# The second norm's shift and scale, moved from the token rows to the transposed rows

## The reference

```python
mod = (silu(c) @ wmod).reshape(4, 6, 1, -1)          # one row of 128 per chunk, six kinds
sa, ca, ga, sb, cb, gb = mod[:, 0], ..., mod[:, 5]
h = layernorm(x) * (1 + ca) + sa
x = x + ga * attention_like(h)      # rmsnorm, gate and value, two depthwise convolutions, fuse, out
h = layernorm(x) * (1 + cb) + sb    # the second norm, with its modulation
x = x + gb * moe(h)                 # 160 experts, the 8 largest weighted, and a shared one
```

## Time and profile before

| | |
|---|---|
| median of 3 runs | 573.82 us (571.63 to 575.61) |
| the profiled execution, its own time | 573.52 us |
| its span, first to last instruction | 571.7 us |
| mean granted TensorE clock | 0.987 of full |
| PE busy | 544.1 us (95% of the span) |
| DVE busy | 474.0 us (83%) |
| ACT busy | 414.4 us (72%) |
| POOL busy | 29.6 us (5%) |

### The profile page before, as it was taken

The page is one execution under the profiler, slowest core; times in us unless marked ns, Lnnn a source line. Parts: engine busy times, 40 slices in busy tenths (PEclk is TensorE's granted clock), DMA queues, the critical chain, the costliest instruction groups (busy, mean ns, idle before and its releaser), DMA issues.

```text
span 571.7 us, 7315 instructions
## 1 busy us (share of the span) xinstructions
PE 544.1 (95%) x2528; PEld 251.4 (44%) x2528; DVE 474.0 (83%) x600; ACT 414.4 (72%) x668; POOL 29.6 (5%) x52
## 2 busy tenths in 40 slices
PE   5697889999999999999999999999989999999996
PEld 3334424543444444454444444454434444444442
DVE  5676479999959988799859688789959988999995
ACT  5446488789777776779666686568876877777773
POOL 5011000050000000011000000002000000000000
PEclk9797999999999999999999999999999999999999
DMA  7976075445534655455544455455635666566650
GB/s 265 346 258 263 10 248 180 150 150 179 185 110 148 204 187 176 146 169 199 158 138 148 170 185 174 148 181 188 213 119 180 231 201 203 198 207 205 200 186 18
DMA packets 33244, 103.26 MB, mean 181 GB/s; under 512 B 3700, under 2 KB 9013, under 8 KB 32952
## 3 DMA queue, kind: packets, MB, share of 16 engines
q1 hardware_dynamic: 33208, 102.81, 53.3%
HBM read 99.90 MB, written 2.37 MB: 179 GB/s over the span
## 4 chain that ended last, share of the span: by engine, by line
PE 78%; DVE 9%; ACT 5%; issue 4%; DMA 2%; POOL 1%; SPq 0%; ACTq 0%; DVEq 0%
PE bank L954 24%; PE bank L955 24%; PE bank L956 24%; DVE g_all L927 2%; DVE s_all L931 2%; PE bank L1075 2%; ACT g_all L667 1%; DMA c_all<-combine 1%; PE bank L1085 1%; DMA g_all<-wmod_dram 1%; ACT s_all L648 1%; DVE w L791 1%; PE bank L1150 1%; ACT hnT L594 1%; PE bank L1109 0%
## 5 line engine op out<-in xcount | busy, mean ns | idle before, releaser
L648 ACT ACTIVATE s_all<-bank 128x512 f32<-128x512 f32 x320 | 189.4, 593 | 109.6 <-PE bank L956 105.9
L927 DVE TENSOR_TENSOR g_all<-s_all,g_all 128x1024 f16<-128x1024 f32 x160 | 195.3, 1221 | 55.6 <-ACT g_all L667 55.1
L931 DVE TENSOR_TENSOR s_all<-s_all,c_all 128x1024 f32<-128x1024 f32 x160 | 194.8, 1218 | 3.9 <-DMA c_all<-combine 3.4
L667 ACT ACTIVATE g_all<-s_all 128x1024 f16<-128x1024 f32 x160 | 168.0, 1050 | 3.4 <-DVE s_all L931 3.3
L954 PE MATMUL bank<-x_h,w 128*128 128x512 f16 x320 | 121.4, 380 | 4.1 <-ACT s_all L648 4.0
L954 PE MATMUL bank<-g_all,w 128*128 128x512 f16 x320 | 121.4, 379 | 2.7 <-DVE g_all L927 2.7
L955 PE MATMUL bank<-g_all,w 128*128 128x512 f16 x320 | 121.3, 379 | 0.0
L956 PE MATMUL bank<-g_all,w 128*128 128x512 f16 x320 | 121.3, 379 | 0.0
L956 PE MATMUL bank<-x_l,w 128*128 128x512 f16 x320 | 121.3, 379 | 0.0
L955 PE MATMUL bank<-x_h,w 128*128 128x512 f16 x320 | 121.3, 379 | 0.0
L954 PEld LDWEIGHTS bank<-x_h,w 128*128 128x128 f16 x320 | 31.3, 98 | 46.9 <-ACT s_all L648 10.0
(11 more groups left out here) (212 smaller groups left out, 367.6 us busy)
## 6 DMA issues: line engine op xcount, KB each, us to landing
c_all<-combine SPq DMA_DIRECT2D x160, 512.0 KB, 3.9
w<-w_dram SPq DMA_DIRECT2D x20, 512.0 KB, 8.9
s_all<-mats_dram SPq DMA_DIRECT2D x1, 1152.0 KB, 7.6
attw<-symT_dram SPq DMA_DIRECT2D x1, 1152.0 KB, 10.3
res<-x_dram SPq DMA_DIRECT2D x4, 256.0 KB, 9.0
combine<-cT SPq DMA_DIRECT2D x4, 256.0 KB, 3.1
out_dram<-res SPq DMA_DIRECT2D x4, 256.0 KB, 2.4
mod<-rows_mod SPq DMA_DIRECT2D x1, 960.0 KB, 6.5
```

The costliest lines, as they stand in the source:

```text
L648: a(sr[J % SRING][:, q * L:(q + 1) * L], U[q][:], ACT.Silu, scale=1.0 / ES).then_inc(s["s_done"], 1)
L667: a(gh[n % GRING], sr[n % SRING], ACT.Copy).then_inc(s["hi_set"], 1)
L927: e.tensor_tensor(gl[n % GRING], sr[n % SRING], gh[n % GRING], ALU.subtract).then_inc(s["lo_set"], 1)
L931: e.tensor_tensor(sr[J % SRING], sr[J % SRING], cr[J % CRING], ALU.mult).then_inc(s["gm"], 1)
```

## The change

Rows 3 and 4 of mod (sb and cb) are no longer formed as rows: `MODC` falls from 5 x 128 to 3 x 128 columns, so the setup's wide matmuls and ACT copies are narrower and fewer, and the DMA through HBM carries 576 KB. sb and cb become columns, beside gb, by two more small matmuls; two small DVE instructions put them in SBUF (`sbc`, `cbc`, 1 added to cb). The steps `h2m` and `h2a` are gone. `xh` now has two ACTIVATEs that read TB with a scale and a bias per partition: one writes a float32 copy `x32`, the other `x_h`; `xl` subtracts in SBUF. In the tables `turn2` goes from 22 to 20, `xh` from 23 to 22, and the first convolution tap from 20 to 19.

```diff
-MODC = 5 * D
+MODC = 3 * D
 REST = {
...
-    17: ("t2a",), 18: ("t2b",), 19: ("h2m",), 20: ("h2a",), 22: ("turn2",), 23: ("xh",), 24: ("xl",), 26: ("logit", "shup"),
+    17: ("t2a",), 18: ("t2b",), 20: ("turn2",), 22: ("xh",), 24: ("xl",), 26: ("logit", "shup"),
...
-TAPS = {20: 1, 21: 1, 22: 1, 23: 1, 24: 1, 25: 1, 27: 2, 28: 2, 29: 1, 30: 1, 31: 1, 32: 1, 33: 1, 34: 1, 35: 1, 36: 1}
+TAPS = {19: 1, 21: 1, 22: 1, 23: 1, 24: 1, 25: 1, 27: 2, 28: 2, 29: 1, 30: 1, 31: 1, 32: 1, 33: 1, 34: 1, 35: 1, 36: 1}
...
     att(0, "t2b")
-    att(0, "h2m")
-    att(0, "h2a")
...
             def rows_of(b):
                 act.wait_ge(s["mod_ps"], 1)
-                a(mod[:, b, 0:512], U0[:], ACT.Copy).then_inc(s["mod_half"], 1)
-                act.wait_ge(s["mod_ps"], 2)
-                a(mod[:, b, 512:MODC], U1[:, 0:MODC - 512], ACT.Copy).then_inc(s["mod_half"], 1)
+                a(mod[:, b, :], U0[:, 0:MODC], ACT.Copy).then_inc(s["mod_half"], 1)
...
-                    a(x_h[b][:], TB[:], ACT.Copy).then_inc(s["xh_set"], 1)
+                    if c == 0:
+                        act.wait_ge(s["cb_set"], 2)
+                    else:
+                        act.wait_ge(s["xl_set"], c)
+                    a(x32[:], TB[:], ACT.Identity, bias=sbc[:, c:c + 1], scale=cbc[:, c:c + 1]).then_inc(s["x32_set"], 1)
+                    a(x_h[b][:], TB[:], ACT.Identity, bias=sbc[:, c:c + 1], scale=cbc[:, c:c + 1]).then_inc(s["xh_set"], 1)
...
-                dve.wait_ge(s["gb_ps"], 1)
+                dve.wait_ge(s["cols_ps"], 1)
+                e.tensor_copy(sbc[:], TB[:, B:2 * B]).then_inc(s["cb_set"], 1)
+                e.tensor_scalar(cbc[:], TB[:, 2 * B:3 * B], 1.0, None, ALU.add).then_inc(s["cb_set"], 1)
...
-                elif n == "h2m":
-                    for i in range(2):
-                        w = slice(2 * i, 2 * i + 2)
-                        dve.wait_ge(s["t2_set"], c * NT + 2 * i + 2)
-                        e.tensor_tensor(h0[:, w], h0[:, w], modr(c, 4, 2), ALU.mult).then_inc(s["hm_set"], 1)
-                elif n == "h2a":
-                    for i in range(2):
-                        w = slice(2 * i, 2 * i + 2)
-                        dve.wait_ge(s["hm_set"], 2 * c + i + 1)
-                        e.tensor_tensor(h0[:, w], h0[:, w], modr(c, 3, 2), ALU.add).then_inc(s["h2_set"], 1)
                 elif n == "xl":
                     b = c % 2
+                    dve.wait_ge(s["x32_set"], c + 1)
                     dve.wait_ge(s["xh_set"], c + 1)
...
-                    e.tensor_tensor(x_l[b][:], TB[:], x_h[b][:], ALU.subtract).then_inc(s["xl_set"], 1)
+                    e.tensor_tensor(x_l[b][:], x32[:], x_h[b][:], ALU.subtract).then_inc(s["xl_set"], 1)
...
-                mm(U0[:], scb[:, b, :], wmod[:, 0:512]).then_inc(s["mod_ps"], 1)
-                mm(U1[:, 0:MODC - 512], scb[:, b, :], wmod[:, 512:MODC]).then_inc(s["mod_ps"], 1)
+                mm(U0[:, 0:MODC], scb[:, b, :], wmod[:, 0:MODC]).then_inc(s["mod_ps"], 1)
...
-                    mm(TB[:, 0:B], wmod[:, MODC:], scb[:, :, 0]).then_inc(s["gb_ps"], 1)
-                    mm(A1[0:B, :], scb[:, :, 0], wmod[:, 0:512])
-                    mm(A2[0:B, 0:MODC - 512], scb[:, :, 0], wmod[:, 512:MODC]).then_inc(s["row_ps"], 1)
+                    mm(A1[0:B, 0:MODC], scb[:, :, 0], wmod[:, 0:MODC]).then_inc(s["row_ps"], 1)
+                    for i, j in enumerate((5, 3, 4)):
+                        last = mm(TB[:, i * B:(i + 1) * B], wmod[:, j * D:(j + 1) * D], scb[:, :, 0])
+                    last.then_inc(s["cols_ps"], 1)
...
-                            pe.wait_ge(s["h2_set"], 2 * c + t // 2 + 1)
+                            pe.wait_ge(s["t2_set"], c * NT + t + 2)
```

More of the change, by code:

```diff
@@ L253, in build @@
         gmag, gsgn = sb("gmag", [P, D]), sb("gsgn", [P, D])
-        gbc, gbm, gbs = (sb(n, [P, B]) for n in ("gbc", "gbm", "gbs"))
+        gbc, gbm, gbs, sbc, cbc = (sb(n, [P, B]) for n in ("gbc", "gbm", "gbs", "sbc", "cbc"))
         res = sb("res", [P, B * NT, D])
@@ L266, in build @@
         x_l = [sb(f"x_l{i}", [P, L], F16) for i in range(2)]
+        x32 = sb("x32", [P, L])
         ss32 = sb("ss32", [INTER, L])
@@ L315, in build @@
             "x_in0 x_in1 x_in2 x_in3 pool_zero pads zs_zero zs_one eps_set one_set scb_set mod_ps mod_half mod_set row_ps row_half row_set "
-            "gb_ps gb_set ak_set bm_set fold1 fold1_sb cols_set fold2 zb_set wz_hi wz_lo fold3 waf_hi waf_lo "
+            "cols_ps cb_set gb_set ak_set bm_set fold1 fold1_sb cols_set fold2 zb_set wz_hi wz_lo fold3 waf_hi waf_lo "
             "wb_ps wb_set sc_ps sc_hi sc_lo nws_set winf_set win_hi win_lo sym_set wc_hi wc_lo rr_set rsg_hi rsg_lo sdw_set table_set "
@@ L319, in build @@
             "conv_ps s_set gate_ps gate_set y_ps gy_set wo_set gob_set u_set gx_set base_set o_ps x2_set stats2 aggr2 ve2_set rstd2_set nb2_set "
-            "t2_set hm_set h2_set h2T_ps xh_set xl_set lg_ps pr_set sh_ps ss_set "
+            "t2_set h2T_ps xh_set x32_set xl_set lg_ps pr_set sh_ps ss_set "
             "mx_set rp_set cw_set sm_set sme_set rs_set cn_set cT_ps cT_set c_out "
@@ L389, in setup @@
                 if n == 20:
-                    sp.wait_ge(s["row_set"], 6)
+                    sp.wait_ge(s["row_set"], 5)
                     sp.dma_start(rowd.rearrange("o (b j) -> (o b) j", b=B - 1), row4[1:B]).then_inc(s["row_out"], 16)
@@ L523, in setup @@
                     act.wait_ge(s["row_ps"], 1)
-                    a(row4[:, 0:512], A1[0:B], ACT.Copy)
-                    a(row4[:, 512:MODC], A2[0:B, 0:MODC - 512], ACT.Copy).then_inc(s["row_half"], 1)
+                    a(row4[:], A1[0:B, 0:MODC], ACT.Copy).then_inc(s["row_half"], 1)
                 elif n == 4:
@@ L690, in gains @@
                 e.tensor_scalar(rw[:, 1, :], rw[:, 1, :], 1.0, None, ALU.add).then_inc(done, 1)
-                e.tensor_scalar(rw[:, 4, :], rw[:, 4, :], 1.0, None, ALU.add).then_inc(done, 1)
                 e.tensor_scalar(sgn, rw[:, 2, :], 0.0, 2.0, ALU.is_ge, ALU.mult).then_inc(done, 1)
-                dve.wait_ge(done, 3)
+                dve.wait_ge(done, 2)
                 e.scalar_tensor_tensor(out=mag, in0=sgn, scalar=-1.0, in1=rw[:, 2, :], op0=ALU.add, op1=ALU.mult)\
                     .then_inc(done, 1)
+                dve.wait_ge(done, 3)
+                e.tensor_scalar(mag, mag, 0.25, None, ALU.max).then_inc(done, 1)
                 dve.wait_ge(done, 4)
-                e.tensor_scalar(mag, mag, 0.25, None, ALU.max).then_inc(done, 1)
-                dve.wait_ge(done, 5)
                 e.scalar_tensor_tensor(out=rw[:, 2, :], in0=sgn, scalar=-1.0, in1=mag, op0=ALU.add, op1=ALU.mult)\
@@ L717, in setup @@
                     dve.wait_ge(s["ld_vec"], 16)
-                    dve.wait_ge(s["mod_half"], 2)
+                    dve.wait_ge(s["mod_half"], 1)
                     gains(mod[:, 0].rearrange("p (j d) -> p j d", d=D), gmag[:], gsgn[:], s["mod_set"])
@@ L772, in mod_ready @@
                 else:
-                    dve.wait_ge(s["mod_set"], 6)
+                    dve.wait_ge(s["mod_set"], 5)
             def gates():
-                dve.wait_ge(s["gb_ps"], 1)
+                dve.wait_ge(s["cols_ps"], 1)
+                e.tensor_copy(sbc[:], TB[:, B:2 * B]).then_inc(s["cb_set"], 1)
+                e.tensor_scalar(cbc[:], TB[:, 2 * B:3 * B], 1.0, None, ALU.add).then_inc(s["cb_set"], 1)
                 e.tensor_scalar(gbs[:], TB[:, 0:B], 0.0, 2.0, ALU.is_ge, ALU.mult).then_inc(s["gb_set"], 1)
@@ L1131, in duo @@
                 if J == 0:
-                    pe.wait_ge(s["mod_half"], 2)
+                    pe.wait_ge(s["mod_half"], 1)
                 if J < ALL and J % DUOS == 0:
```

## The result

| | before | after |
|---|---|---|
| median of 20 runs each | 572.83 us (571.31 to 575.61) | 576.35 us (573.77 to 579.66) |
| the profiled execution, its own time | 573.52 us | 578.59 us |
| its span | 571.7 us | 576.8 us |
| mean granted clock | 0.987 | 0.985 |

The account below looks back on a forecast made before the run. PE's order of work was taken to bound the loop, one chain through all engines the prologue. Setup -0.1, prologue xh +0.4, tap +1.85 and +1.4 gave +3.5 us on 573.5, so 577.0 us, range 573.2 to 581.5.

Parts of the forecast that it names:

- The bound: In the loop PE's order of work sets the time; DVE or ACT work counts only through a wait of PE.
- The removal: Four DVE operations per chunk go, 6 us in all; costed at 0, giving only spare time on DVE.
- The setup: Before the first norm: narrower row matmuls start ACTIVATEs 0.8 us earlier, mostly waited away at symT's DMA; -0.1 us.
- xh in the prologue: Prologue chain: two ACTIVATEs of 0.78 us before x_l let PE go on later; +0.4 us.
- xh in the loops: ACT does 1.36 us instead of 0.5 per chunk, within its spare time; 0, bound +0.87 per chunk.
- The tap: First tap at 19 makes PE wait for hnT: net +1.85 us in chunk 0's loop, +1.4 in chunk 1's.
- The give-back of 0.4: Chunk 0's loop: PE's old 0.4 us wait at 137.85 for ACT's silu goes, as ACT catches up during the stall.
- The first, the fall of the clock: Half clock follows chunk 0's new stall, costing 3.4 us more: 580.4 us; chance 0.25.
- The second rival: The tap's stalls cost nothing, because ACT and DVE pace chunk 0 and lost time comes back: 573.8 us; chance 0.11.
- The third, ACT as the bound: ACT's 0.87 us more per chunk at xh is paid in all three loops: 579.6 us; chance 0.06.

Follow-up runs that it names:

- e7: The kernel before without the steps h2m and h2a, everything else in its place; 571.85 us, ratio 0.9999.
- e1: The changed kernel with its first convolution tap put back from behind duo 19 to behind duo 20; 571.72 us, ratio to before 1.0003.
- e5: The changed kernel with the tap at 20, turn2 back at 22 and xh back at 23; 572.86 us, ratio to before 1.0012.
- e6: The changed kernel with the tap at 20 and a third, unread ACTIVATE at xh in the loops; 572.32 us, ratio to before 1.0008.
- e2: The kernel before with only its first convolution tap moved from behind duo 20 to 19; 576.21 us, ratio 1.0071.
- a2: The changed kernel unaltered, profiled once more for the clock; 578.73 us.
- e4: The changed kernel with the early tap in chunk 1's loop alone, in chunk 0's behind duo 20; 573.66 us, ratio to before 1.0036.
- e9: The changed kernel with the tap at 20 and weight pieces moved to later duos of chunk 0; 570.95 us, ratio to before 0.9979.
- e3: The changed kernel with the tap at 20 and x_h made by DVE from x32 instead of by ACT; 571.81 us, ratio to before 1.0003.
- e10: The kernel before with weight pieces moved to later duos of chunk 0, h2m and h2a kept; 570.10 us, ratio 0.9961.

## Why the prediction was right

**The bound.** That PE's order sets the time of the loop held: every microsecond of the loss is a late start on PE, and 6 us less on DVE (e7) moved no stage of it.

**The removal, 0.** Shown by e7, to within some 1 us.

**The setup, -0.1.** Local rows agree: 0.75 us won ahead of `symT`'s wait, and +0.02 at `hr_h` instead of -0.1.

**xh in the prologue, +0.4.** Measured 0.62. The two ACTIVATEs took 0.78 and 0.77 as worked out, overlapped by 0.1, and x_l ended at 63.47 instead of 63.41. What the sum lacked is 0.2 us behind it: before, the first logit matmul came behind taps that were still running, now PE stands waiting and starts 0.21 after x_l's end. A wait for a producer has to be booked with its start behind it.

**xh in the loops, 0.** Chunk 1 and 2 are unchanged in e1 and e5. The room was read a little too large, as e6 showed, without harm here.

**The tap, +1.85 and +1.4.** This is the term that carried the forecast. Stalls forecast at 2.25 and 1.4, measured 2.28 and 1.40. The give-back of 0.4 was right in size (0.44), and its cause, ACT catching up during the stall, is borne out by e2. What I missed is that `turn2` at 20 removes the same wait with no stall at all (e1 against e5), where I had written that its "own time only moves". In the changed kernel either would do, so the sum is the same; against e1, where that wait is gone already, the stall costs its full 2.28.

**The rivals.** The first, the fall of the clock, came true in its mechanism in all three profiled executions that had the long stall (after, a2, e2), and was oversized. Duos 19 to 23 are 3.78 us longer than in e1; 2.28 are the stall, so the half clock cost 1.50, not 3.4. I had taken the length of the fall from the earlier trace rows, 7.4 us in the prologue; behind this stall it was 3.4 us. Denser matmuls are not needed to explain that: the stall of 1.88 us in the prologue is in all 14 profiled executions, and the half clock behind it lasts 6.8 us in three of them (before, after, a2), 3.4 us in ten, and in e5 it does not come. I had gone by one execution. PE in e5, the window behind it, and the window over the fall in e1:

```profile
46.74 2.05 PE L1078 MATMUL bank<-wo,attw 128*128 128x128 f32 x16 [1.88 <-DVE attw L862]
```

```profile
46.00:53.40 7.40, 5.09 (x36) 3.45 (x37) 3.85 (x16) 3.12 (x8) 2.42 (x4) 1.00 0.76 309
```

```profile
47.00:55.00 8.00, 6.83 (x38) 5.05 (x39) 3.25 (x14) 3.33 (x8) 1.72 (x3) 0.79 0.57 233
```

The fall did not come behind the 1.2 us idle in chunk 1 (after, a2, e2, e4), nor behind the 1.64 us of the earlier trace rows in any of the 14. The Trainium skill (TensorE: Matmul & The Clock Gate, A second HAM failure mode: psum-queue depth-cycling) tells of a kernel whose frequent short idles between groups of matmuls made the clock go down and up. Here the fall came once, behind one stall of 2.1 us that had idle times of 1.05 and 0.64 us in the 11 us before it; e1 has these two alone and keeps 1.00. Whether the 2.1 us would do it without them was not tried.

Whether the fall comes in every execution isn't shown. The changed kernel's 20 runs have a mean clock of 0.983 to 0.994, 0.989 on average, e1's twelve 0.994 on average; one fall of 3.4 us takes off 0.003. That speaks for it in most of them, but the prologue's falls are in the same number, and the chips differ. Without the fall the loop's part would be +3.2 us, with it +4.7; the ratio's interval, 2.6 to 4.6 us, lies about between. The profiled execution was a poor stand-in for the median, 2.2 us above it, and the loop is not all of that: its duo 0 starts at 73.49 (a2: 73.47), in the five executions with the same prologue and the tap elsewhere (e1, e4, e5, e6, e9) at 70.8 to 72.0. Why stays open.

The second rival, stalls that cost nothing, is refuted by the ledger: beyond the wait at duo 21 nothing of them is given back in the duos behind them. The third, ACT as the bound, is refuted by e1 and e5. By the Trainium skill (ScalarE: Activation LUTs, Rules for kernel authors) an add and a multiply belong on VectorE; e1 shows no loss in the total from the opposite. No run has the arithmetic back on DVE in the new layout; e3 moves a cast alone, which shortens the prologue's chain by 0.28 us locally and nothing in total.

So the mechanism was right, and the closeness of the number is in part luck. The forecast was +3.5 us, the timed runs have +3.6. The terms as measured in the profiles (0.62, 0.02, 2.28 - 0.44 and 1.40) give +3.9 without the fall of the clock, which the forecast left out, and +5.4 with it. The timed runs' interval ends below the second, at 4.6; whether that is because some executions lack the fall is not settled.

## What to carry to other kernels

Where engines run one written order, look first at which steps moved relative to the step of another engine that they wait for: one number in a table cost 3.6 us, while moving all of the modulation's arithmetic cost nothing that could be measured. To price such a move, set the consumer's earliest start beside the producer's end in the trace, and add the engine's restart behind the wait; if the stall is new and longer than those that the trace shows with a full clock behind them, add some microseconds at half clock as a case of its own, and take their length from more than one execution. And the busy share of an engine, 81% here, does not say where it holds another up: 6 us less on DVE gave nothing (e7), while other pieces of work, moved out of the few duos where the backlog reached PE, gave some 2 us (e10).

## What the runs showed of the hardware

- An idle time of 2.1 us of PE between dense matmuls was followed by 3.4 us at half clock in the three profiled executions that had it. In the changed kernel it starts some 0.6 us behind the restart at 136.72 (0.64 in the window from 137 is half clock for 0.72 of it), with 1.00 again from 141; in e2 some 0.9 us behind the restart at 134.87 (0.91 in the window from 135).
- The same stall of PE, 1.88 us in the prologue, was followed by 6.8 us at half clock in three profiled executions, by 3.4 us in ten and by none in one. One trace does not give the price of a fall.
- An ACTIVATE of 128x512 out of PSUM takes 0.78 us with two operands per partition (0.78 and 0.77 in the changed kernel) and 0.60 with none.
- DVE casts 128x512 from float32 to float16 in SBUF in 0.43 us, against 0.69 for a subtraction of the same size (both in e3).
